# Moving the prenorm's scale-and-shift from ScalarE to VectorE in a four-block transformer kernel

## The reference

```python
x = x + _layernorm(_L0_attn_ref(_layernorm(x), ...))   # latent attention with rope, causal, 16 heads
x = x + _layernorm(_L0_ffn_ref(_layernorm(x), ...))    # ternary-weight FFN 1024 -> 4096 -> 1024
x = x + _layernorm(_L1_attn_ref(_layernorm(x), ...))   # spectrally filtered attention, 16 heads
x = x + _layernorm(_L1_ffn_ref(_layernorm(x), ...))    # q, k, v by routed leaf MLPs, then attention
```

```python
def _layernorm(x, axis=-1, eps=1e-5):
    m = jnp.mean(x, axis=axis, keepdims=True)
    v = jnp.var(x, axis=axis, keepdims=True)
    return (x - m) / jnp.sqrt(v + eps)
```

## Time and profile before

| what | us |
|---|---|
| median of the runs shown (2 runs) | 11747.47 |
| lowest and highest of them | 11727.16, 11767.79 |
| the profiled execution, its own time | 11774.13 |
| its span on the slowest core (core 6) | 11772.6 |
| the span of the fastest core (core 0) | 11678.0 |

### The profile page before, as it was taken

One profiled execution on the slowest core, in us unless ns is written; L12 is line 12 of the kernel. 1 busy time (PEld: TensorE's weight loads), 2 busy tenths in 40 slices (PEclk: granted clock), 3 DMA queues, 4 the chain that ended last, 5 costly groups with the idle time before them and its releaser, 6 DMA issues.

```text
span 11772.6 us, 98398 instructions; the slowest of 8 cores (11678.0 to 11772.6 us)
## 1 busy us (share of the span) xinstructions
PE 7623.5 (65%) x30918; PEld 2861.1 (24%) x31200; DVE 1984.3 (17%) x3826; ACT 3748.5 (32%) x5097; POOL 1024.5 (9%) x1559
## 2 busy tenths in 40 slices
PE   5677315555678886475656776666666888736566
PEld 2111102332211111343432111233321111124343
DVE  3011541111100002311123111211110000231122
ACT  2455201111245554121223454311123555411122
POOL 0100001111010000101001100111102000010100
PEclk7555657877755556686776555778775555658777
DMA  1000343222100000000001000223210000000000
GB/s 42 3 3 3 105 166 115 90 88 88 22 1 2 2 2 9 15 15 19 26 29 14 2 3 10 70 92 99 91 24 6 2 2 2 9 16 15 17 13 15
DMA packets 238489, 397.07 MB, mean 34 GB/s; under 512 B 27937, under 2 KB 172321, under 8 KB 234914
## 3 DMA queue, kind: packets, MB, share of 16 engines
q0 software_dynamic: 72784, 184.71, 6.2%
q1 hardware_dynamic: 165202, 206.05, 5.6%
HBM read 403.41 MB, written 33.56 MB: 37 GB/s over the span
## 4 chain that ended last, share of the span: by engine, by line
PE 53%; DVE 12%; DMA 11%; ACT 11%; issue 7%; POOL 4%; DVEq 1%; ACTq 0%; POOLq 0%; SPq 0%
PE pall L109 52%; ACT pt L119 6%; DMA arena<-w2q_dram 4%; ACT arena L119 4%; POOL pt L130 3%; DVE st L157 3%; DVE arena L130 2%; DVE arena L139 1%; DVE stream L130 1%; DMA arena<-l0f_w2T 1%; DVE arena L154 1%; ACT pall L119 1%; PE pall L115 1%; DVE arena L142 1%; DVE st L130 1%
## 5 line engine op out<-in xcount | busy, mean ns | idle before, releaser
L109 PE MATMUL pall<-arena 128*128 128x256 bf16 (+7 forms) x19158 | 4626.2, 390 | 1755.6 <-ACT arena L119 546.3
L109 PEld LDWEIGHTS pall<-arena 128*128 128x128 bf16 (+2 forms) x19360 | 1805.2, 108 | 4396.0 <-issue 3818.0
L119 ACT ACTIVATE pt<-pall,cbias 128x1024 bf16<-128x1024 f32 (+7 forms) x2048 | 1924.7, 940 | 1868.4 <-PE pall L109 1845.2
L109 PE MATMUL pall<-pt,arena 128*65 128x512 bf16 (+5 forms) x6016 | 2076.1, 461 | 439.4 <-DVE pt L130 182.9
L119 ACT ACTIVATE arena<-pall 128x256 bf16<-128x256 f32 (+3 forms) x1162 | 535.6, 461 | 2789.2 <-PE pall L109 2677.9
L109 PEld LDWEIGHTS pall<-pt,arena 128*65 128x65 bf16 (+2 forms) x6016 | 560.3, 123 | 1891.4 <-issue 1833.4
L130 POOL TENSOR_TENSOR pt<-arena 128x256 bf16<-128x256 bf16 (+2 forms) x656 | 668.5, 1019 | 2822.0 <-ACT arena L119 2305.1
L109 PE MATMUL pall<-pt,ones 128*1 128x256 bf16 (+2 forms) x896 | 341.8, 436 | 420.4 <-ACT pt L119 262.3
L130 DVE TENSOR_TENSOR arena<-pall,pt 64x1024 bf16<-64x1024 f32 x128 | 155.8, 1217 | 2528.2 <-ACT pt L119 2521.5
L109 PE MATMUL pall<-arena,pt 128*128 128x512 bf16 (+2 forms) x2032 | 417.8, 345 | 148.6 <-ACT pt L119 118.1
L115 PE MATMUL pall<-ident,pt 128*128 128x128 bf16 x1284 | 157.2, 307 | 537.7 <-DVE pt L146 192.6
(11 more groups left out here) (105 smaller groups left out, 3065.0 us busy)
## 6 DMA issues: line engine op xcount, KB each, us to landing
arena<-wfcq_dram SPq DMA_DIRECT2D x128, 1024.0 KB
arena<-w2q_dram POOLq DMA_DIRECT2D x128, 512.0 KB, 4.1
arena<-l0f_wfcT POOLq DMA_DIRECT2D x8, 2048.0 KB, 10.0
arena<-l0f_wfcT SPq DMA_DIRECT2D x8, 2048.0 KB
arena<-l0f_w2T SPq DMA_DIRECT2D x32, 512.0 KB
arena<-l0f_w2T POOLq DMA_DIRECT2D x32, 512.0 KB, 4.3
stream<-x_in SPq DMA_DIRECT2D x16, 512.0 KB
stream<-x_in POOLq DMA_DIRECT2D x16, 512.0 KB, 4.0
```

The lines of the kernel that those rows point to most:

```text
L109: return t.matmul(out, lhsT, rhs, start=start, stop=stop)
L119: self.do("scalar", lambda s: s.activation(out, in_, func, bias=bias, scale=scale, accum_out=accum_out), wait=wait, inc=inc)
```

## The change

Step 1 is taken from ScalarE and given to VectorE, in both branches of `emit_prenorm_fm`: one `tensor_scalar` (helper `ts`, L142 for two operations) with the two columns `rstd` and `negmur` as its operands replaces the activation. Input, output, shapes and the place in the program are the same; the marks that others wait on now count VectorE's semaphore.

```diff
         if lo_cb is None:
-            p.act(hi_tm, h.stream[:, t, :], AF.Identity,
-                  bias=negmur[:, t:t + 1], scale=rstd[:, t:t + 1],
-                  wait=p.need(f"{tag}_rstd{t // 4}", f"{tag}_nm{t // 4}",
-                              f"{tag}_cast{par}", f"{tag}_tp{par}"),
-                  inc="act")
-            p.mark(f"{tag}_cast{par}", "act")
+            p.ts("vector", hi_tm, h.stream[:, t, :], rstd[:, t:t + 1],
+                 negmur[:, t:t + 1], ALU.mult, ALU.add,
+                 wait=p.need(f"{tag}_rstd{t // 4}", f"{tag}_nm{t // 4}",
+                             f"{tag}_cast{par}", f"{tag}_tp{par}"),
+                 inc="dve")
+            p.mark(f"{tag}_cast{par}", "dve")
         else:
-            p.act(f32t[:, :], h.stream[:, t, :], AF.Identity,
-                  bias=negmur[:, t:t + 1], scale=rstd[:, t:t + 1],
-                  wait=p.need(f"{tag}_rstd{t // 4}", f"{tag}_nm{t // 4}",
-                              f"{tag}_cast{par}"), inc="act")
-            p.mark(f"{tag}_f32{par}", "act")
+            p.ts("vector", f32t[:, :], h.stream[:, t, :], rstd[:, t:t + 1],
+                 negmur[:, t:t + 1], ALU.mult, ALU.add,
+                 wait=p.need(f"{tag}_rstd{t // 4}", f"{tag}_nm{t // 4}",
+                             f"{tag}_cast{par}"), inc="dve")
+            p.mark(f"{tag}_f32{par}", "dve")
             p.copy("vector", hi_tm, f32t[:, :],
                    wait=p.need(f"{tag}_f32{par}", f"{tag}_tp{par}"),
                    inc="dve")
```

## The result

The changed kernel takes 11897.48 us (median of 11 runs, 11878.12 to 11957.05), the kernel before on the same chip 11752.45 us (median of 10 runs, 11708.83 to 11774.45). The ratio is 1.0135, with an interval of 1.0116 to 1.0155. That is slower by 1.35% of 11752, or 159 us, and within 2%. The forecast was +160 and 11908 us.

What follows compares the result with a forecast made beforehand. ScalarE was taken to pace blocks 1 and 2's passes at about 1.33 us a tile, VectorE block 3's. Terms 96 + 35 + 29 = +160 us on the 11747.5 us median gave 11908 us, range 11870 to 11962.

Steps and rivals of the forecast that it cites:

- the likeliest case: All eight passes: a chain of one tile after another at 812 ns or close, +160 us, 11908 us; chance 0.87.
- The duration: The new VectorE scale-and-shift in all passes: 812 ns, taken from the nearest row, with ends 753 and 1226 ns.
- The rival of 1226 ns: All passes: VectorE's instruction is slow, as in the residual addition; +53 us more, so +213 and 11961 us; chance 0.06.
- The order: VectorE's queue: the next scale-and-shift stands behind the copy waiting for transposes, so a tile takes 2.95 us against 1.33.
- Blocks 1 and 2: Their four prenorm passes: 47.2 us instead of 23.2, +24.0 each, +96 in all.
- Block 0: Its two passes: six groups +4.2 us each, +25, and the first groups' later tiles +10; together +35.
- Block 3: Its two passes, paced by VectorE: 0.81 us and a 0.11 gap added to each of 32 tiles, +29 us.
- VectorE +104: Busy time over the kernel: VectorE's grows by 104 us and ScalarE's falls by 159.
- Hidden passes: Behind the passes: a late transfer's wait hides their growth, +0, about 11745 us; chance 0.02.
- TensorE's clock: Behind every pass: the clock rises later, 9.4 us a pass, 75 in all, +235, 11983 us; chance 0.03.
- The 19 us: Behind every pass, in the clock rival: the assumed delay of the clock's rise, at half the speed.
- estimate of 698 ns: The new instruction: (158 + 512) / 0.96 GHz from the skill page, which would make the sum 15 us smaller.

Runs made afterwards that it cites:

- experiments 3 and 4: 3: kernel before, each scale-and-shift also waits for previous tile's copy, ratio 1.0152; 4: changed kernel, next tile's scale-and-shift ahead of copy, block 3 as before, ratio 1.0026.
- experiment 5: Changed kernel with one GpSimd memset of the ones columns held back until block 2's prenorm pass is over; one run of 11928.66 us.
- b3_ahead: Kernel before, with block 3's cast and remainder of tile t+1 written ahead of tile t's bias additions on VectorE; 11662.42 us, ratio 0.9905.

## Why the prediction was right

**The result** is the likeliest case, +159 by the ratio against +160, inside the range of 11870 to 11962. The two medians alone lie 145 apart; both kernels scatter by tens of us, so an agreement to 1 us is partly luck. The trace is the better witness, at +164 from the passes on its core and in the mean of all eight.

**The duration.** Taken as 812 ns, the nearest row; it is 814 (median) with bf16 output and 812 with f32. The rival of 1226 ns is out. What the text left open, column or output type, is now decided for the output: with two columns the bf16 output costs the same as the f32 one. That leaves the second column instead of the constant for the 60 ns between 753 and 812, but the rows also differ in the arithmetic operation (a comparison and an addition in the row of 753, a multiplication and an addition in the other), and no run separates the two.

**The order.** The sum of 2.95 us for a tile is what the timeline shows, and experiments 3 and 4 show the cause from both sides: the order without the engine loses more than the change (56.04 us for a pass), the engine without the order loses 5.3 us in block 1's pass (28.52 - 23.20), where the change lost 24.3.

**The terms.** Blocks 1 and 2: +96 predicted, +98.1 found, of which 1.8 are the long instruction in one pass of block 2. The prediction had no term for that meeting with GpSimd; that it is small is luck, and the last section shows it on the other cores. Block 0: +35 and +35.2. Block 3: +29 and +30.7; 28.3 of it lie between the first copy and the end of the last, where 30 tiles of 0.92 would give 27.6, and the rest lies between the statistics and the first copy. VectorE +104 predicted and +106 found, ScalarE -159 and -155.

**The rivals.** Hidden passes: the passes grew by 164.0 us in the mean of all cores and the spans by 160.7, so next to nothing of the growth was hidden. TensorE's clock: windows behind block 2's pass in the changed kernel, against the earlier trace rows:

```profile
3062.00:3067.00 5.00, 5.00 (x16) 1.83 (x15) 0.00 (x0) 0.44 (x2) 0.00 (x0) 0.63 0.01 3
3067.00:3073.00 6.00, 6.00 (x29) 2.69 (x28) 2.45 (x2) 0.00 (x0) 0.00 (x0) 0.97 0.00 0
```

The granted clock is 0.63 in the first five us and 0.97 in the next six, where it was 0.50 and 0.95. TensorE was at its lower level (1.2 GHz) through the pass in both kernels, and rose no later behind a pass that was twice as long and half as busy. The price of this rival, 9.4 us a pass, isn't there: in all it would be 75 us, and the time outside the passes has not grown. The 19 us that this price rests on were assumed in the prediction and come from no row. Its 0.50 "in the passes" is shown for blocks 1, 2 and 3, not for the start of block 0.

## What to carry to other kernels

Before a step is moved to an engine with more idle time, look at what the step's own consumers have in that engine's queue. Here VectorE was idle for more than half of the pass, but the copy that waits for the tile's transposes stood ahead of the next tile's step, so a faster instruction (0.81 for 1.24 us) gave a tile of 2.95 us instead of 1.33. If a step has to be there, write that of tile t+1 ahead of the waiting instruction of tile t, and compare the engine's load per tile with the old pace first: 1.71 us was still more than 1.33. And where the queue of the pacing engine already holds a wait ahead of work that is ready, as in block 3, turning those two round made the kernel about 1% faster (ratios 0.9905 and 0.9885), while both orders of the moved step gave a loss or nothing.

## What was not expected of the hardware

**An instruction three times as long beside GpSimd.** The longest scale-and-shift of the changed kernel, in block 2's pass of the first sequence:

```profile
3017.05 0.90 POOL L126 DMA_DIRECT2D arena<-l_wv  x1 [1.94 <-DMA arena<-c_dfts]
3017.14 2.60 DVE L142 TENSOR_SCALAR pt<-stream,st 128x1024 bf16<-128x1024 f32 x1
3017.94 1.25 POOL L167 MEMSET arena<- 128x256 bf16 x1
...
8744.10 1.26 POOL L167 MEMSET arena<- 128x256 bf16 x1
...
8744.26 0.69 DVE L154 COPY arena<-pall 128x1024 bf16<-128x1024 bf16 x1 [1.33 <-PE pall L115]
8745.06 0.84 DVE L142 TENSOR_SCALAR pt<-stream,st 128x1024 bf16<-128x1024 f32 x1
```

It starts 0.09 us after GpSimd's DMA issue and ends at 3019.74, 0.55 us after the memset's end at 3019.19. On ScalarE, where the step was before, all 96 took 1239 to 1242 ns. The last three lines are the second sequence's pass. There the copy out of PSUM runs beside the memset and keeps its 0.69 us, and the scale-and-shift meets only the memset's end: it takes 0.84 us and again ends 0.55 us after the memset (8745.90 and 8745.36). The memset stretches one scale-and-shift in each of the 16 block 2 passes of the eight cores, 13 of them to about 2.2 us or more, and each ends 0.55 us after the memset. The passes of block 1, which have no memset, take 47.48 and 47.13 us on this core, this one of block 2 49.27. With the memset moved behind the pass (experiment 5), the same place reads:

```profile
2998.11 0.90 POOL L126 DMA_DIRECT2D arena<-l_wv  x1 [3.33 <-DMA arena<-c_dfts]
2998.50 1.00 DVE L142 TENSOR_SCALAR pt<-stream,st 128x1024 bf16<-128x1024 f32 x1
```

The 2.60 us are gone, the pass takes 47.70, and 1.00 instead of 0.81 us beside the DMA issue alone is left. So most of the delay is the memset's and a small part goes with the issue: this instruction ends 0.49 us after the issue's end (2999.50 and 2999.01). Over the eight cores of that run the longest scale-and-shift in block 2 takes 1.18 us, and one beside an issue in block 0 takes 1.23. How long a meeting lasts depends on when GpSimd's transfers land. The cost is 1.8 us on this core and 1.8 to 3.5 on the eight.

The Trainium skill, "SBUF — State Buffer" (section "Who interferes with whom"), states that VectorE's copy, cast and scale-and-shift can run in modes that take the port pair shared with GpSimd, that whoever comes first holds it for its whole instruction, and that ScalarE waits for nobody. By that rule the trace agrees: 2.60 against 0.81 us on VectorE, and 1239 to 1242 ns on ScalarE. The move from ScalarE to VectorE is then also a move onto that pair.

The same meeting shows in block 3, from the other side. In the kernel before, GpSimd's comparison of a tile's last sums (TENSOR_SCALAR, 128x15) runs beside VectorE's cast of the next tile, which takes 0.69 us from 4735.12:

```profile
4735.23 0.69 POOL L139 TENSOR_SCALAR arena<-st 128x15 bf16<-128x15 f32 x1 [0.56 <-DVE st L130]
4741.92 0.25 POOL L139 TENSOR_SCALAR arena<-st 128x15 bf16<-128x15 f32 x1 [5.99 <-DVE st L130]
```

It ends at 4735.92, 0.11 us after the cast, where the next one, with no cast beside it, takes 0.25. In b3_ahead the cast lies elsewhere, and all three comparisons of a tile are short:

```profile
4783.66 0.26 POOL L139 TENSOR_SCALAR arena<-st 128x15 bf16<-128x15 f32 x1 [3.74 <-DVE st L130]
4784.48 0.26 POOL L139 TENSOR_SCALAR arena<-st 128x15 bf16<-128x15 f32 x1 [0.56 <-DVE st L130]
4785.30 0.26 POOL L139 TENSOR_SCALAR arena<-st 128x15 bf16<-128x15 f32 x1 [0.56 <-DVE st L130]
```

In the kernel before, 14 comparisons of this pass are long ones, and 14 x 0.43 = 6.0 us is what GpSimd's busy time fell by. In the changed kernel the comparison meets the scale-and-shift instead and takes 0.82 us. Nobody waited for this comparison, so it cost nothing in any of these kernels.

**The second column.** 812 to 814 ns with two statistics columns, whether the output is f32 or bf16, and 753 (bf16 output) with one and a constant. The prediction's estimate of 698 ns from the Trainium skill, "VectorE: DVE Perf Modes" (section "Side-by-side: where the cycles go for N=2048 bf16"), is 114 short of the row; the measurement decides.
